# A state-space scan stage on VectorE: self-waits named one by one, and the state product cut in four

## The reference, cut to what matters

```python
def step(h, inp):                       # h: [B, 2048, 16]
    dt_t, B_t, C_t, u_t = inp
    dA = jnp.exp(dt_t[:, :, None] * A)
    h = dA * h + (dt_t * u_t)[:, :, None] * B_t[:, None, :]
    y = jnp.einsum('bdn,bn->bd', h, C_t)
    return (h, y)
```

## Time and profile before

| what | value |
|---|---|
| median of 3 runs | 24686.26 us (24684.4 to 24740.88) |
| profiled execution, its own time | 24702.78 us |
| its span, slowest core (core 7) | 24701.2 us |
| spans of the 8 cores | 24631.9 to 24701.2 us |
| DVE busy | 14589.4 us, 59% of the span |
| PE busy / PE weight load busy | 8352.1 us, 34% / 3615.3 us, 15% |
| ACT busy | 7143.4 us, 29% |
| DMA queues, share of 16 engines | 15.0% and 1.0% |
| mean granted TensorE clock | 0.645 of full speed |

### The profile page before, as it was taken

How to read it: one execution, slowest core, us unless ns; L and a number is a source line. 1 busy time by engine, 2 the same in 40 slices (tenths; PEclk the granted TensorE clock), 3 DMA queues, 4 the chain that set the end, 5 groups by cost and what they waited for, 6 DMA issues and landing times.

```text
span 24701.2 us, 148005 instructions; the slowest of 8 cores (24631.9 to 24701.2 us)
## 1 busy us (share of the span) xinstructions
PE 8352.1 (34%) x35298; PEld 3615.3 (15%) x35298; DVE 14589.4 (59%) x15169; ACT 7143.4 (29%) x10162; POOL 69.0 (0%) x134
## 2 busy tenths in 40 slices
PE   0003333343333333433333433333333433333334
PEld 0002011220022100220012200221002201121102
DVE  0445766557664667457665576546674576645775
ACT  0001443123421344114431234213431144312341
POOL 1000000000000000000000000000000000000000
PEclk9996555665566655765566655665556655576556
DMA  6222001220022100320012200221002200022002
GB/s 134 71 63 63 7 19 28 62 61 12 15 51 69 30 19 7 81 65 5 19 28 64 61 13 13 55 72 24 19 12 75 65 5 20 26 75 49 20 5 65
DMA packets 1906519, 1015.82 MB, mean 41 GB/s; under 512 B 1387633, under 2 KB 1797873, under 8 KB 1905666
## 3 DMA queue, kind: packets, MB, share of 16 engines
q1 hardware_dynamic: 1887074, 971.23, 15.0%
q0 software_dynamic: 18592, 35.14, 1.0%
HBM read 972.67 MB, written 68.68 MB: 42 GB/s over the span
## 4 chain that ended last, share of the span: by engine, by line
DVE 41%; PE 24%; ACT 15%; DMA 10%; issue 7%; DVEq 1%; SPq 1%; ACTq 0%; POOL 0%; POOLq 0%
DVE mHTA L172 11%; DVE mUB L172 8%; PE mps_y L172 6%; PE fps_m L172 5%; PE mps_m L172 5%; ACT mAEX L172 4%; ACT mT L172 3%; ACT mBCREP L172 3%; PE mps_bc L172 3%; DVE fVQ L172 2%; DMA fWPa<-w2q 2%; PE aps_m L172 2%; DVE fMXG L172 2%; DVE fCQ L172 1%; DVE fHQ L172 1%
## 5 line engine op out<-in xcount | busy, mean ns | idle before, releaser
L172 DVE TENSOR_TENSOR_SCAN mHTA<-mAEX,HST,mUB 128x512 bf16<-128x512 f32 x4096 | 5257.9, 1284 | 1500.3 <-ACT mAEX L172 908.7
L172 PE MATMUL mps_y<-mUB,IDE 128*128 128x512 bf16 x4096 | 1909.7, 620 | 6721.7 <-DVE mUB L172 6721.7
L172 ACT ACTIVATE mAEX<-mDT,ATL 128x512 f32<-128x512 bf16 x4096 | 2956.3, 722 | 1304.0 <-DVE mHTA L172 871.0
L172 ACT CAST mBCREP<-mps_bc 128x1024 bf16<-128x1024 f32 x1024 | 1036.3, 1012 | 3708.2 <-PE mps_bc L172 3360.0
L172 PEld LDWEIGHTS mps_y<-mUB,IDE 128*128 128x128 bf16 x4096 | 443.4, 126 | 8161.5 <-issue 8161.5
L172 DVE TENSOR_TENSOR mUB<-mWT,mBCREP 128x2048 bf16<-128x2048 bf16 x1024 | 1254.2, 1225 | 174.6 <-DVE mUB L172 160.2
L172 PE MATMUL fps_m<-fHQ,fWPa 128*128 128x256 bf16 x4096 | 680.1, 345 | 1899.0 <-DVE fHQ L172 1537.6
L172 DVE TENSOR_TENSOR mUB<-mHTA,mBCREP 128x2048 bf16<-128x2048 bf16 x1024 | 1254.3, 1225 | 110.7 <-DVE HST L172 5.7
L172 ACT ACTIVATE fHG<-fHG,FV 128x256 f32<-128x256 f32 x1024 | 518.8, 508 | 2557.8 <-DVE fHG L172 2557.3
L172 DVE TENSOR_TENSOR fHG<-fps_m,fAREP 128x256 f32<-128x256 f32 x1024 | 434.5, 424 | 927.7 <-PE fps_m L172 927.3
L172 DVE TENSOR_TENSOR mDT<-mT,mT 128x512 bf16<-128x512 f32 x256 | 177.0, 692 | 1283.4 <-ACT mT L172 1283.4
(11 more groups left out here) (194 smaller groups left out, 13184.9 us busy)
## 6 DMA issues: line engine op xcount, KB each, us to landing
fWPa<-w1q SPq DMA_DIRECT2D x256, 512.0 KB, 4.5
fWPb<-w1q SPq DMA_DIRECT2D x256, 512.0 KB, 4.6
fWPa<-w2q SPq DMA_DIRECT2D x256, 512.0 KB, 5.9
fWPb<-w2q SPq DMA_DIRECT2D x256, 512.0 KB, 6.5
mWINZ<-inwb SPq DMA_DIRECT2D x64, 1024.0 KB, 5.2
mWOU<-outwb SPq DMA_DIRECT2D x256, 256.0 KB, 3.8
wq_in<-w1t SPq DMA_DIRECT2D x128, 256.0 KB, 2.8
wq_in<-w2t SPq DMA_DIRECT2D x128, 256.0 KB, 2.8
```

The lines of the kernel that those rows point to most:

```text
L172: ins = getattr(eng, meth)(*a, **kw)
```

## The change

The tile sizes, the buffers and the arithmetic stay. Three things change in the scan stage.

- A flag `relax` is on during the stage. With it `tensor_tensor_scan`, `tensor_tensor` and `tensor_copy` are recorded without any fence. Where an operation needs a result of its own engine, the code names it: `selfwait(e, tok)` waits for the token of that one operation, and is left out when a later one was already waited for.
- `m` is cut into four operations of 128x512, one for each block.
- The order on VectorE is new. `wb` of iteration `kk+1` is issued within iteration `kk`; the first two pieces of `m` lie between the scans.

The diff, its core:

```diff
+            if ctx.relax and meth in ("tensor_tensor_scan", "tensor_tensor",
+                                      "tensor_copy"):
+                fi = _FakeIns()
+                ctx.log.append((nm, meth, a, kw, fi))
+                return fi
...
+    def selfwait(self, e, tok):
+        if tok is None:
+            return
+        pe, val = tok
+        assert pe == e
+        if self.fcnt[e] >= val:
+            return
+        self.e[e].wait_ge(self.sem[e], val)
+        self.fcnt[e] = val
...
-                        c.wait("v", reps_tok[sl], prev_mq[pq], prev_yacc[pq])
-                        c.inc("v", v.tensor_tensor(
-                            out=seg(wbq, 4, TC),
...
-                        for di in range(4):
+                        c.selfwait("v", save_tok[0])
+                        c.selfwait("v", wb_tok[kk])
+                        c.wait("v", prev_mq[pq], prev_yacc[pq])
...
+                        def emit_m(di):
+                            c.selfwait("v", tts_tok[di])
+                            return c.inc("v", v.tensor_tensor(
+                                out=mq[:, di * TC:(di + 1) * TC],
+                                in0=HTA[:, di * TC:(di + 1) * TC],
+                                in1=Cq, op=ALU.mult))
+
+                        emit_tts(0)
+                        emit_tts(1)
+                        emit_m(0)
+                        emit_tts(2)
+                        emit_m(1)
+                        emit_tts(3)
+                        if kk + 1 < KTOT:
+                            emit_wb(kk + 1)
+                        if kk + 2 < KTOT:
+                            issue_bc(kk + 2)
+                        c.selfwait("v", tts_tok[3])
                         c.inc("v", v.tensor_copy(
...
-                        mvq = c.inc("v", v.tensor_tensor(
-                            out=seg(mq, 4, TC), in0=seg(HTA[:, 0:Q4], 4, TC),
-                            in1=fbc(Cq, 4, TC), op=ALU.mult))
+                        save_tok[0] = c.tok("v")
+                        emit_m(2)
+                        mvq = emit_m(3)
```

More of the change, by code:

```diff
@@ L215, in inc_fence @@
         return tk
+    relax = False
+    def selfwait(self, e, tok):
[7 more added lines that the diff above has]
+        self.fcnt[e] = val
     def dma(self, qe, stream, out, in_, **kw):
@@ L1214, in issue_bc, with emit_wb @@
                     evac_last[0] = ev
+                c.relax = True
+                wb_tok = {}
+                save_tok = [None]
+                KTOT = 4 * NST
+                def emit_wb(kk2):
+                    pq2 = kk2 % 2
+                    sl2 = kk2 % 3
+                    goff2 = (kk2 // NST) * 4
+                    wbq2 = WB[:, (2 * pq2) * Q4:(2 * pq2) * Q4 + Q4]
+                    Bq2 = BCREP[:, sl2 * 2 * TC: sl2 * 2 * TC + TC]
+                    c.wait("v", reps_tok[sl2])
+                    wb_tok[kk2] = c.inc("v", v.tensor_tensor(
+                        out=seg(wbq2, 4, TC),
+                        in0=WTl[:, :].rearrange("p (b w) -> p b w", b=DIB)
+                        [:, goff2:goff2 + 4, :],
+                        in1=fbc(Bq2, 4, TC), op=ALU.mult))
                 for g4 in range(4):
@@ L1224, in emit_mamba, with emit_tts @@
                             issue_bc(1)
-                        Bq = BCREP[:, sl * 2 * TC: sl * 2 * TC + TC]
+                            c.wait("v", prep_done)
+                            emit_wb(0)
                         Cq = BCREP[:, sl * 2 * TC + TC: sl * 2 * TC + 2 * TC]
+                        mq = WB[:, (2 * pq + 1) * Q4:(2 * pq + 1) * Q4 + Q4]
                         wbq = WB[:, (2 * pq) * Q4:(2 * pq) * Q4 + Q4]
-                        mq = WB[:, (2 * pq + 1) * Q4:(2 * pq + 1) * Q4 + Q4]
-                        c.wait("v", reps_tok[sl], prev_mq[pq], prev_yacc[pq])
-                        c.inc("v", v.tensor_tensor(
-                            out=seg(wbq, 4, TC),
-                            in0=WTl[:, :].rearrange("p (b w) -> p b w", b=DIB)
-                            [:, goff:goff + 4, :],
-                            in1=fbc(Bq, 4, TC), op=ALU.mult))
-                        for di in range(4):
+                        c.selfwait("v", save_tok[0])
+                        c.selfwait("v", wb_tok[kk])
+                        c.wait("v", prev_mq[pq], prev_yacc[pq])
+                        tts_tok = [None] * 4
+                        def emit_tts(di):
                             dib = goff + di
@@ L1248, in emit_mamba @@
                                 op0=ALU.mult, op1=ALU.add))
-                            aex_used[di] = c.tok("v")
-                        if kk + 2 < 4 * NST:
+                            tts_tok[di] = c.tok("v")
+                            aex_used[di] = tts_tok[di]
+                        def emit_m(di):
[13 more added lines that the diff above has]
+                        if kk + 2 < KTOT:
                             issue_bc(kk + 2)
+                        c.selfwait("v", tts_tok[3])
                         c.inc("v", v.tensor_copy(
@@ L1278, in emit_mamba @@
                     c.wait("t", c.tok("v"))
+                c.relax = False
             scan_done = c.tok("v")
```

## The result

| | before | changed |
|---|---|---|
| median | 24705.49 us (8 runs) | 23173.56 us (8 runs) |
| profiled execution, own time | 24702.78 us | 23177.39 us |
| its span | 24701.2 us, core 7 | 23175.8 us, core 3 |

The ratio is 0.9377, 95% interval 0.9367 to 0.9388: 6.2% faster. The gain was 1.53 ms instead of 1.32.

A forecast was written before the change was run, and what follows sets the result against it. VectorE bounds the scan stage by its operations and the gaps between them. Savings of 1254 + 64 + 12 - 15 = 1315 us from 24702.78 give 23388 us, forecast as 23380 us; range 23280 to 24260 us, 82%.

The forecast's parts named there:

- without a wait the distance from start to start is the length less 0.08 us: VectorE operations with no wait overlap the one ahead; each removed gap gives about 0.18 us, 0.25 with two waits.
- steps 1 to 3 of the sum: Mid-group iteration: scans 4.80 us, m 1.38, wb 1.145 and save 0.10, together 7.43 against 8.83.
- something that I called rare: Longer gaps on VectorE in the scan stage; their vanishing was allowed for only in the likeliest case's lower end, 23300 us.
- The gate: Around `z_group`, wb no longer runs in VectorE's pause for nothing: loss 0.24 x 64 = 15 us.
- the group ends: Group end with another behind: 13.18 us falls to 11.84, saving 1.34 x 48 = 64 us.
- The range: Whole kernel's time: 23280 to 24260 us, 82%, taking in the first rival and a little on both sides.
- The rival that priced them: Scan-stage waits in VectorE's queue are only taken when the engine is idle: 24820 us, 0.5% slower; chance 8%.
- the one without overlap: Scan-stage VectorE operations have no gap, but no overlap either: 24210 us; chance 10%.
- the one in which the narrow pieces slow down: Pieces of m run at f32 pace, 0.692 us each, 1.07 us more per iteration: 24480 us; chance 5%.
- the strict reading of the Trainium skill: No VectorE operation starts before the one ahead is finished, waits or no waits: 25380 us; chance 3%.
- ScalarE was in time: Mid-group, next iteration's first exponential is done at +5.10 us, its scan comes at +7.35; 2.25 us remain.
- The busy sum of VectorE: Sign to look for in the profile: it rises by about 490 us although the span falls.

The follow-up runs named there:

- eight pieces: The changed kernel with m cut into eight pieces of 128x256 instead of four of 128x512: 23435.38 us.
- waits alone: Against the kernel before: fences off, only true needs waited for, old order, m whole: 23369.65 us, ratio 0.9458.
- order and cut alone: Against the kernel before: new order and m in four pieces, but every scan-stage VectorE operation waits for the one just ahead: 25598.65 us, ratio 1.0363.

## Why the prediction was wrong, point by point

**The step that failed** is "without a wait the distance from start to start is the length less 0.08 us", as a size, with which steps 1 to 3 of the sum were made. It gave 7.43 us; the iteration has 7.25:

| | forecast | measured, start to start (medians) |
|---|---|---|
| four scans | 4.80 | 4.76 |
| four pieces of m | 1.38 | 1.30 |
| wb | 1.145 | 1.116 |
| save | 0.10 | 0.071 |

Two parts make the 0.17. The overlap was rounded down: 0.085, for the save 0.10, over ten operations 0.06 us. And the lengths were those of operations that had waited; in the chain they are shorter, 4 x 8 + 4 x 13 + 22 + 4 ns by the mean lengths above, 0.11 us. Both could be read beforehand: the copy behind the scan in the earlier trace rows lasts 0.13, the other one 0.15, and from the second copy to `aM` are 0.07, while I put 0.10 for the save. The groups of before say the same of f32 products of 512 (mean ns): 692 behind a wait, 681 and 684 without one.

```profile
L172 DVE TENSOR_TENSOR aSA<-aP,aM 128x512 f32<-128x512 f32 x64 | 44.3, 692 | 6.7
...
L172 DVE TENSOR_TENSOR aSB<-aT,aM 128x512 f32<-128x512 f32 x64 | 43.8, 684 | 0.0
L172 DVE TENSOR_TENSOR aM<-aP,aT 128x512 f32<-128x512 f32 x64 | 43.6, 681 | 0.0
```

Over 896 iterations the 0.17 to 0.18 us are 160 us. The tests with eight pieces and with waits alone show this shortening in other chains.

**28 us more** in mid-group, and about 25 of them are something that I called rare and left out of the sum. The mean iteration before was 8.862, not 8.834, since some gaps were longer, most of them 0.53 us instead of 0.17. Such gaps are there again where bare waits are put back (0.53 us ahead of a scan, in the version with order and cut alone); in the changed kernel all 896 mid-group iterations are within 0.06 us of the median. They aren't chance. Of the 82 gaps over 0.28 us in mid-group on core 7 of the kernel before, 80 stand at the same operation on each of the other seven cores. One of them on core 7, then on core 0, the third scan of iteration `kk` = 44 in the first scan stage:

```profile
3036.36 1.28 DVE L172 TENSOR_TENSOR_SCAN mHTA<-mAEX,HST,mUB 128x512 bf16<-128x512 f32 x1 [0.53 <-DVE mHTA L172]
```
```profile
3036.99 1.28 DVE L172 TENSOR_TENSOR_SCAN mHTA<-mAEX,HST,mUB 128x512 bf16<-128x512 f32 x1 [0.53 <-DVE mHTA L172]
```

So they belong to places in the program. What causes them there stays open; no run isolates it. The gate (-5 instead of -15) and the group ends (74 for 64) follow from the shorter iteration.

**The range** failed with it. It reached 880 us up to the rivals but only 100 down, since I had taken the forecast's own rule as the lower bound. The trace of before had no scan-stage operation in a chain, so the distances should have been bounded below as well: the copy's 0.03 us (0.13 against 0.15 in length, 0.07 against 0.10 in distance) on each of ten operations in 1024 iterations is 300 us.

**What was right.** Waits on earlier work are taken ahead, at no cost in nearly all mid-group iterations (the test with 30 more: 7.252 us by the median, 0.01 more by the mean). The rival that priced them, the one without overlap, and the one in which the narrow pieces slow down (412 ns, not 692) are out. So is the strict reading of the Trainium skill ("VectorE: DVE Perf Modes", section "The DRAIN you can't avoid"), by which no operation starts before the one ahead is finished and semaphores cost nothing: operations in a chain start 0.085 us before that, and the same ten operations take 7.25 us with named waits and 9.63 with a wait for each one ahead. The Trainium skill's advice to keep the number of operations low ("VectorE: DVE Perf Modes", section "Rules for kernel authors") holds beside it: the cut costs 0.21 us. ScalarE was in time, though I had misread its rows a little: an exponential lasts 0.72 us and they start 0.87 apart, where I took 0.82 for both. The busy sum of VectorE fell by 508 us where I had it rise by 490. That doesn't speak against the mechanism: the page of the profile counts overlapping stretches once (4096 scans of 1276 ns are 5226 us, its busy time for them 5139). Count times mean length, over the scan stage's four kinds, rose by about 374 us.

## What to carry to other kernels

On an engine that is the bound, look at the gaps of 0.1 to 0.2 us: each wait for the operation just ahead cost about 0.2 us here, and one independent operation in between removed it. Cut an operation only as far as the data need it: each cut cost 0.07 us in the chain (0.21 for three, 0.27 for the four more that make eight pieces), and writing to a second half of the buffer, which allows m whole, cost nothing. Lengths measured with waits were upper bounds for the chain without them, so a range worked out from them must reach below.

## What the runs showed of the hardware that was not expected

An operation of VectorE without a bare wait starts 0.085 us before the recorded end of the one ahead (behind the 128x4 save 0.10) and is itself recorded shorter: 25 ns less right behind a scan (from its start to the next one's 1.175 us, against 1.201 for a scan behind a bare wait), 4 to 8 ns less behind other kinds (1.195). Thirty satisfied waits added in 7.25 us left the median mid-group iteration as it was and made the mean 0.01 us longer. A bf16 product right behind a scan took, from its start to the next one's, 0.183 us for 256 elements, 0.317 for 512, and 1.116 for 2048. Where waits are bare, the longer gaps come at the same places of the program on all eight cores, 80 of 82 in the kernel before.
